# Instruction orders of the first two tiles, engine by engine, in a fused recurrent and linear-attention layer

## The reference

```
x = x + tanh(g0) * wkv(decay, first, k=layernorm(x), v=ctx)     # per channel recurrence over time
h = silu(x_prev*conv0 + x*conv1)          # on layernorm(x); "prev" is along the batch axis
q = silu(h @ Wq);  k = h @ Wk;  v = h @ Wv;  g = h @ Wg         # 512, 512, 1024, 1024 columns
q, k = rotary(q), rotary(k);  logits = v . router -> softmax over 2, argmax routes q and k
o = tril(q_routed @ k_routed.T) @ v  per head (16 heads);  o = normalise per head
x = x + tanh(g1) * (silu(g) * o) @ Wout
```

## Time and profile before

| what | us |
|---|---|
| median of 3 runs | 1667.74 (1665.98 to 1668.46) |
| profiled execution, device time | 1668.04 |
| its span, first to last instruction | 1666.3 |
| TensorE busy in the span | 1580.1 |
| VectorE busy in the span | 1503.6 |
| ScalarE, GpSimd busy | 735.2, 715.2 |
| mean granted TensorE clock | 0.981 |

### The profile page before, as it was taken

The page is one execution under the profiler, slowest core; times in us unless marked ns, Lnnn a source line. Parts: engine busy times, 40 slices in busy tenths (PEclk is TensorE's granted clock), DMA queues, the critical chain, the costliest instruction groups (busy, mean ns, idle before and its releaser), DMA issues.

```text
span 1666.3 us, 37489 instructions
## 1 busy us (share of the span) xinstructions
PE 1580.1 (95%) x15770; PEld 817.6 (49%) x15770; DVE 1503.6 (90%) x1990; ACT 735.2 (44%) x973; POOL 715.2 (43%) x710
## 2 busy tenths in 40 slices
PE   3567899999999999999999999999999999999997
PEld 2523355555555455555554555555545555555453
DVE  6787899999999999999999999999999999999942
ACT  4765534444443344444433444444334444443320
POOL 1123245544445455444454554444545544445431
PEclk9788999999999999999999999999999999999999
DMA  8500011111111111111111111101111111010001
GB/s 263 199 11 14 15 37 40 39 39 32 26 34 27 38 40 40 39 30 29 35 28 38 40 40 39 32 25 35 27 38 40 40 39 31 27 35 28 26 14 26
DMA packets 23296, 69.73 MB, mean 42 GB/s; under 512 B 2248, under 2 KB 2520, under 8 KB 23128
## 3 DMA queue, kind: packets, MB, share of 16 engines
q1 hardware_dynamic: 23128, 67.33, 13.9%
HBM read 50.55 MB, written 16.78 MB: 40 GB/s over the span
## 4 chain that ended last, share of the span: by engine, by line
PE 76%; DVE 2%; issue 0%; ACT 0%; DVEq 0%
PE ps_g L416 23%; PE ps_g L417 22%; PE ps_g L420 22%; PE ps_o L620 3%; PE ps_s L605 2%; PE ps_o L408 1%; PE ps_t L408 1%; PE ps_t L564 1%; PE ps_t L572 0%; PE ps_t L581 0%; PE ps_s L577 0%; DVE fb L1040 0%; DVE seg L1047 0%; DVE fb L1057 0%; DVE x_ring L1190 0%
## 5 line engine op out<-in xcount | busy, mean ns | idle before, releaser
L416 PE MATMUL ps_g<-big,h_hi 128*128 128x512 f16 x1536 | 586.0, 382 | 14.7 <-DVE big L1002 7.0
L420 PE MATMUL ps_g<-big,h_lo 128*128 128x512 f16 x1536 | 585.8, 381 | 0.0
L417 PE MATMUL ps_g<-big,h_hi 128*128 128x512 f16 x1536 | 585.7, 381 | 0.0
L416 PEld LDWEIGHTS ps_g<-big,h_hi 128*128 128x128 f16 x1536 | 156.1, 102 | 185.6 <-issue 19.3
L420 PEld LDWEIGHTS ps_g<-big,h_lo 128*128 128x128 f16 x1536 | 150.8, 98 | 183.5 <-issue 3.9
L417 PEld LDWEIGHTS ps_g<-big,h_hi 128*128 128x128 f16 x1536 | 150.9, 98 | 164.3 <-issue 3.6
L1446 POOL TENSOR_TENSOR small<-small 128x1 f32<-128x1 f32 x64 | 12.1, 189 | 490.0 <-DVE small L1030 480.5
L1465 POOL TENSOR_TENSOR vx<-vx,ek 128x1024 f32<-128x1024 f32 x32 | 76.0, 2376 | 309.3 <-DVE fa L1040 295.5
L416 PE MATMUL ps_g<-big 128*128 128x512 f16 x512 | 196.3, 383 | 5.7 <-DVE big L1134 5.6
L417 PE MATMUL ps_g<-big 128*128 128x512 f16 x512 | 195.6, 382 | 0.0
L420 PE MATMUL ps_g<-big 128*128 128x512 f16 x512 | 195.3, 381 | 0.0
(11 more groups left out here) (179 smaller groups left out, 2800.7 us busy)
## 6 DMA issues: line engine op xcount, KB each, us to landing
x_ring<-in_x SPq DMA_DIRECT2D x32, 512.0 KB
vx<-in_ctx SPq DMA_DIRECT2D x32, 512.0 KB
out<-x_ring SPq DMA_DIRECT2D x31, 512.0 KB
big<-in_wv SPq DMA_DIRECT2D x2, 2048.0 KB, 15.6
big<-in_wg SPq DMA_DIRECT2D x2, 2048.0 KB, 17.9
big<-in_wout SPq DMA_DIRECT2D x2, 2048.0 KB, 18.1
big<-in_wq SPq DMA_DIRECT2D x1, 2048.0 KB, 19.8
big<-in_wk SPq DMA_DIRECT2D x1, 2048.0 KB, 24.0
```

The source lines that it names most:

```text
L416: nc.tensor.matmul(dst[:, :], hi, hi_of(u)[:, kc * HALF:(kc + 1) * HALF], start=(kc == 0), stop=False)
L417: nc.tensor.matmul(dst[:, :], hi, lo_of(u)[:, kc * HALF:(kc + 1) * HALF], start=False, stop=False)
L420: last = nc.tensor.matmul(dst[:, :], lo, hi_of(u)[:, kc * HALF:(kc + 1) * HALF], start=False, stop=(kc == KC - 1))
```

## The change

No instruction is added or taken away. On TensorE, bound_row(2) and (3) come later among the blocks; in step 0 q's first half goes ahead of bound_row(4), k is no longer cut by bound_row(6), bound_row(7) cuts g0, and bound_row(8) moves from the middle of the second tile's k to behind the first tile's scores. q's first half gets a wait for lo_block(14) of its own. On ScalarE, q's split goes ahead of k's bound sum; o0's bound sum and the second tile's silu and split go ahead of the first tile's second gate; o0's split goes ahead of the second tile's q. On VectorE the spreads, scales and low parts are put in the order that goes with this, and `denominator_scan` is cut in two functions so that spread(3) can stand between them.

```diff
@@ -453,15 +453,16 @@
                 last.then_inc(s_vm, 1)
 
             def first_step():
+                unit_ready(UQ)
+
+                pe.wait_ge(s_vlo, 2 * KC - 1)
+                project(ps_g[0], h_hi, h_lo, UQ, s_qp, 0)
                 bound_row(4)
-                unit_ready(UQ)
-                project(ps_g[0], h_hi, h_lo, UQ, s_qp, 0)
+                project(ps_g[0], h_hi, h_lo, UQ, s_qp, 1)
                 bound_row(5)
-                project(ps_g[0], h_hi, h_lo, UQ, s_qp, 1)
                 unit_ready(UK)
-                project(ps_g[1], h_hi, h_lo, UK, s_kp, 0)
+                project(ps_g[1], h_hi, h_lo, UK, s_kp)
                 bound_row(6)
-                project(ps_g[1], h_hi, h_lo, UK, s_kp, 1)
                 pe.wait_ge(s_rw, 4)
                 pe.wait_ge(s_tc, 10)
                 route_products(0)
@@ -473,15 +474,17 @@
                 unit_ready(UV + 1)
                 pe.wait_ge(s_k, 1)
                 project(ps_g[1], h_hi, h_lo, UV + 1, s_vp)
-                bound_row(7)
                 unit_ready(UG)
                 pe.wait_ge(s_vc, 1)
-                project(ps_g[0], h_hi, h_lo, UG, s_gp)
+                project(ps_g[0], h_hi, h_lo, UG, s_gp, 0)
+                bound_row(7)
+                project(ps_g[0], h_hi, h_lo, UG, s_gp, 1)
                 xn_transposes(1, True)
                 unit_ready(UG + 1)
                 pe.wait_ge(s_vc, 2)
                 project(ps_g[1], h_hi, h_lo, UG + 1, s_gp, None, lambda: scores_ready(0))
                 scores(0)
+                bound_row(8)
                 for g in range(2):
                     values_ready(0, g)
                     values(0, g)
@@ -499,10 +502,7 @@
                 if main:
                     route_products(i)
                     bank_free(i, 1, prev2)
-                    project(ps_g[1], h_hi, h_lo, UK, s_kp, 0)
-                    if i == 1:
-                        bound_row(8)
-                    project(ps_g[1], h_hi, h_lo, UK, s_kp, 1)
+                    project(ps_g[1], h_hi, h_lo, UK, s_kp)
                     route_logits(i)
                     after(pe, s_q, i + 1)
                     project(ps_g[0], h_hi, h_lo, UV, s_vp, 0)
@@ -649,11 +649,10 @@
                 turn_block(m)
                 if m == 2:
                     bound_row(1)
-                if m == 6:
+                if m == 9:
                     bound_row(2)
-                if m == 9:
                     xn_transposes(0, False)
-                if m == 14:
+                if m == 2 * KC - 1:
                     bound_row(3)
                 if m:
                     centre_block(m - 1)
@@ -794,11 +793,12 @@
                 split_unit(5)
                 normed_x(1, 1)
                 silu_gate(0, 0)
-                silu_gate(0, 1)
-                exp_k(2, 2)
+                bound_unit(6)
                 silu_h(1)
                 split_h(1, 0)
                 split_h(1, 1)
+                silu_gate(0, 1)
+                exp_k(2, 2)
 
             def step(i, slot, main, nxt, nxt2, prev, prev2):
                 n, p = i + 1, i - 1
@@ -807,7 +807,7 @@
                         after(act, s_op, 2 * p + g + 1)
                         A(squares[:, g * HALF:(g + 1) * HALF], ps_o[g][:, :], ACT.Square).then_inc(s_sq, 1)
                 if i == 1:
-                    bound_unit(6)
+                    split_unit(6)
                 if main:
                     copy_q(i)
                 if i == 1:
@@ -815,8 +815,6 @@
                 if main:
                     copy_logits(i)
                     copy_k(i)
-                if i == 1:
-                    split_unit(6)
                 if main:
                     route_prob(i)
                 if nxt:
@@ -942,12 +940,12 @@
             split_centred(12)
             copy_turned(15)
             split_centred(13)
+            split_unit(2)
+            split_centred(14)
             bound_unit(3)
-            split_centred(14)
             split_centred(15)
-            split_unit(2)
+            split_unit(3)
             seed(1)
-            split_unit(3)
             pipeline(step, first_step)
 
 
@@ -1079,21 +1077,18 @@
                     out_scale(p)
                 if main:
                     rotate_q(i)
-                if i == 1:
-                    spread(8)
                 if nxt:
                     numerator_terms(n)
                 if main:
                     signs(i)
                 if i == 1:
-                    set_scale(8)
+                    lo_unit(6)
                     spread(9)
                 if i == 1:
                     set_scale(9)
                     for g in range(2):
                         V.tensor_scalar(base[:, g:g + 1], mx[:, UO + g:UO + g + 1], tg[:, 1:2], HEAD_BOUND / G_TOP,
                                         ALU.mult, ALU.mult).then_inc(s_base, 1)
-                    lo_unit(6)
                 if nxt:
                     numerator_scan(n)
                 if i == 1:
@@ -1197,9 +1192,15 @@
                 recurrence_turn(n, ek[:, :], carry_b, s_sva, s_ekt)
                 first_terms(n, s_ekt, fa[:, :], s_fda)
 
+            def denominator_pass(n):
+                scan(n, s_fda, s_sca, carry_b, s_sva)
+
+            def denominator_add(n):
+                add_state(fa[:, :], s_den)
+
             def denominator_scan(n):
-                scan(n, s_fda, s_sca, carry_b, s_sva)
-                add_state(fa[:, :], s_den)
+                denominator_pass(n)
+                denominator_add(n)
 
             def numerator_turn(n):
                 dve.wait_ge(s_ev, n + 1)
@@ -1334,21 +1335,23 @@
                 lo_unit(4)
                 recurrence_output(1)
                 output_transpose(1)
+                spread(7)
                 residual(1, 1)
-                spread(7)
+                set_scale(7)
                 route_coefficients(0)
-                set_scale(7)
                 turn_heads(s_rk, 0, rot_k, k_sb, s_kt)
                 turn_heads(s_route, 0, route, sgn_t, s_rt)
                 same(0)
+                first_norm(2, 2)
                 lo_unit(5)
-                first_norm(2, 2)
                 conv_products(1, 0)
                 conv_products(1, 1)
                 conv_sum(1)
+                spread(8)
                 mask(0)
+                set_scale(8)
+                h_low(1)
                 gate_scale(0)
-                h_low(1)
 
             for cols, value in ((nhalf, -0.5), (eps_c, EPS), (dv_c, 1.0 / DV), (shift1, -SHIFT), (shift2, 0.0)):
                 V.memset(cols, value).then_inc(s_cv, 1)
@@ -1400,8 +1403,8 @@
             output_transpose(0)
             lo_block(3)
             residual(0, 0)
+            spread(2)
             lo_block(4)
-            spread(2)
             first_norm(1, 1)
             lo_block(5)
             set_scale(2)
@@ -1417,18 +1420,19 @@
             lo_block(10)
             denominator_terms(1)
             lo_block(11)
-            denominator_scan(1)
+            denominator_pass(1)
             spread(3)
+            denominator_add(1)
             lo_block(12)
             set_scale(3)
             numerator_turn(1)
             lo_block(13)
+            lo_unit(2)
+            lo_block(14)
+            numerator_terms(1)
             spread(4)
-            numerator_terms(1)
-            lo_block(14)
+            set_scale(4)
             lo_block(15)
-            lo_unit(2)
-            set_scale(4)
             route_bound()
             spread(5)
             lo_unit(3)
```

## The result

The changed kernel takes 1657.89 us (median of 4 runs, 1655.55 to 1658.22), the kernel before 1667.43; the ratio is 0.994 with a 95% interval of 0.9923 to 0.9958. A later set of runs, beside some of the experiments, gave 1657.42 (1655.44 to 1657.94) and 0.9933 (0.992 to 0.9946); beside it the kernel before took 1667.50, the median of its eight runs in the fast state, with one of 3312 us left out. The profiled execution took 1658.22 us with a span of 1656.4, which is 9.8 less than the 1668.04 of before. The forecast was 1653 us, in a range of 1646 to 1661: the direction and the range hold, 14.9 us of gain were summed and 9.8 came.

What follows compares the result with a forecast made beforehand. TensorE was taken as full from the second tile on, so its earlier waits cost kernel time one for one. A lead of 12.7 us at out unit 0 plus 2.2 for its warm half gave 14.9: 1668.04 to 1653.1, range 1646 to 1661.

Steps and rivals of the forecast that it cites:

- The early part: Up to signs(0) in the first tile: reordered bound rows, spreads and q's split, 4.7 us of gain left at signs(0).
- correction, rotation and signs (4.4) as before: VectorE behind bound_row(6) and its scale in the first tile: 4.4 us, unchanged, so signs(0) ends at 107.05, not 111.79.
- The second term: g1's projection in the first tile: 24 matmuls priced at 7.4 us, bounds 5.2 and 10.2, old 7.0.
- VectorE's stretch: Second tile, mask(0) to out unit 0: 49.8 us without the stops, 51.3 with GpSimd contention added, against 59.05 before.
- The last item: Out unit 0's first half in the second tile: TensorE arrives busy, 2.6 us instead of 4.8, 2.2 more gain.
- the forecast's own signs: Right: second tile's q at 139 to 140; wrong: over 1 us wait before the out unit, VectorE's queue longer than summed.
- the loop kept its 47.60 us: Rival, slower loop: GpSimd contention makes VectorE need 48.2 us a step, 31 steps lose 19 us, 1672 us; chance 0.04.
- GpSimd did not go first for a whole step: Rival, second tile: lo_unit(6) waits out 22.58 us of GpSimd work, starts at 166.1; 1662 us, chance 0.04.
- less comes through: Rival: cold stretches at upper bounds (k and g1 10.2 us each), gain falls by 5.5, partly hidden; 1657 to 1660, chance 0.20.

Runs made afterwards that it cites:

- The early part alone: Only the change up to the first tile's k (bound_row(2) to (6), spreads 2 to 5, q's split), rest as in the kernel before: 1663.62 us, ratio 0.997.
- The later part: Run alone on the kernel before: spread(7), first_norm, bound rows 7 and 8, o0's sums and split, second tile's silu, lo_unit(6) before spread(9); 1661.99 us, ratio 0.9963.

## Why the prediction was right, with a gain 5 us too large

Step by step, the new times as forecast and as in the trace after:

| point | forecast | trace | before |
|---|---|---|---|
| q starts | 80.9 | 81.70 | 90.52 |
| k starts | 94.0 | 94.57 | 98.4 |
| k ends, bound_row(6) | 101.5 | 102.23 | 104.62 (in the middle of k) |
| signs(0) done | 107.05 | 110.78 | 111.79 |
| g1 starts | 127.6 | 131.23 | 132.86 |
| scores(0) | 135.0 | 139.43 | 139.82 |
| mask(0) to first gated low half | 51.3 long | 51.2 long | 59.05 long |
| out unit 0 | 187.7 | 192.11 | 200.36 |

The early part was right in its waits: 3.92 us at set_scale(4) where I had 4.3, 4.99 before k where I had 4.7, and the slow k with 7.7 us where I had taken 7.5. The 0.8 us by which q is late stand already behind h_low(0): GpSimd's product started at 61.41, not at 60.4, h_low took 3.41 us beside it (2.99 in the old trace), and lo_block(10) started at 64.88, not at 63.9.

The step that failed is "correction, rotation and signs (4.4) as before". They took 7.5 us (103.31 to 110.78). I had priced GpSimd against VectorE in the second tile and not here, where the old trace had them apart: there GpSimd's rotation began at 110.24, in the last 0.4 us of VectorE's. With bound_row(6) behind all of k, the end of k releases both in the same moment. This is a term of the sum that was mis-sized by 3.1 us; with the rotations apart the same stretch takes 4.7 us (103.08 to 107.78). "SBUF — State Buffer" (Who interferes with whom) of the Trainium skill says that a VectorE instruction with two SBUF inputs contends with a GpSimd one that reads SBUF; the trace agrees here (L1238, 2.31 us for 1.22) and at lo_unit(6) (6.17 us against 4.8). I named it for the second tile only, and should have asked after each new start of a GpSimd operation.

The second term is g1. I took 7.4 us and it was 8.2; the clock was lower for 14 matmuls, behind idle stretches of 5.0 and 2.6 us where I had 3.6 and 2.9. More to the point, I had accepted the slow g1 as given. The old order had 7.0 with 8 slow matmuls and a g0 without any (idle 2.8 ahead of g0, 0.5 and 1.3 ahead of g1). The early part alone had 5.3: 5.3 us of idle and the slow matmuls lay on g0, for which nobody waits. The later part moves idle time from ahead of g0 to ahead of g1, the projection that the scores, mask and all of VectorE wait for. The forecast had the longer idle stretches and kept nearly the old price.

3.7 us at signs(0) less 0.1 in VectorE's stretch and 0.8 at g1 make 4.4 us at the scores (139.43 for 135.0), and the same 4.4 at the out unit. The second tile was right to 0.1 us in VectorE's stretch, in part by luck: numerator_terms(2), for which I had 2.87 us, took 1.18, and the loss came one instruction later, in signs(1), where L1159 took 1.68 us for 0.18. The 7.4 us stop at bound_row(9) was foreseen and, as the run with spread(9) first shows, without a price. The last item, the out unit's warm first half, is there: 2.6 us instead of 4.8. The lead then stands at 10.4 us in the loop (scores at 1000.64 and 1011.06) and at 9.9 at the end of the span; where the last half microsecond goes I did not follow.

Two of the forecast's own signs did not come as stated. The second tile's q stood at 145.55 and not at 139 to 140: 4.4 us were carried over from the scores, and values took the rest, with a stop of 1.2 us within them. And there was a wait of 1.55 us before the out unit, above the 1 us that was to mean a longer queue on VectorE. That queue was as long as summed (51.2 us); it was TensorE's that was shorter, mainly since the second half of v had 7 slow matmuls and not 12, and its scores(1) came 3.0 us later than forecast while VectorE came 4.4 later.

Of the rivals, the loop kept its 47.60 us, and GpSimd did not go first for a whole step: lo_unit(6) started at 160.86 and took 6.17 us. The time fell where the case "less comes through" had it, 1657 to 1660, but for another reason in the main: of the 4.4 us missing at the out unit, 3.1 are the collision with GpSimd, and the slow stretches that the case names give 1.0 (k 0.2, g1 0.8).

## What to carry to other kernels

When an order of instructions makes two engines start on the same event, price them as slowing each other, from a row in which they met, and look for a wait that keeps them apart if one has slack. When idle time of TensorE is moved, ask which projection comes next behind it: slow matmuls are free on one that nobody waits for and cost everything on one that all wait for; matmuls that nobody reads can fill the stretch. A scale that other engines wait for goes in front of a burst as soon as its input is there, not behind it.

## What the runs showed of the hardware

- A VectorE instruction of 0.2 us can last until a GpSimd instruction ends: L1159 (128x16) took 1.68 us in the second tile of each trace of the new order, against 0.18 in the first tile of the changed kernel. It ended at 160.95, and GpSimd's L1508, which had begun at 157.94, at 160.92.
- The number of slow matmuls behind a wait is not fixed. Behind the same 3.58 us wait q's first twelve had 12, 10, 9 and 7 matmuls at the lower clock in executions of kernels that are the same up to there, and q began between 80.3 and 81.7 us. In the two traces of the changed kernel bound_row(4), behind these twelve, stands at 86.39 and 84.65: 1.7 us of their difference are made there.
- 20 unread matmuls (4.48 us), which left 0.67 us of a 5.0 us wait, kept the granted clock up: no slow one in the 24 behind them. "TensorE: Matmul & The Clock Gate" (What's actually happening) of the Trainium skill says that the array's clock follows how busy it has been; the trace agrees, with 12 slow matmuls of 24 without and none with the fill.
